# Second norm, choice of expert and scatter as one stage by batches of 1024 tokens, and gates chosen inside the second attention

## The reference

```python
probs = jax.nn.softmax(mla_out @ router_w + router_b, axis=-1)
topw, topi = jax.lax.top_k(probs, TOPK)                    # TOPK = 2
topw = topw / (topw.sum(-1, keepdims=True) + 1e-08)
combine = jnp.sum(jax.nn.one_hot(topi, E, dtype=probs.dtype) * topw[..., None], axis=-2)
h1 = jax.nn.gelu(jnp.einsum('bsd,edf->ebsf', mla_out, w1) + b1[:, None, None, :], approximate=False)
h2 = jnp.einsum('ebsf,efd->ebsd', h1, w2) + b2[:, None, None, :]
return hs + 0.3 * jnp.einsum('bse,ebsd->bsd', combine, h2)
```

```python
for i in range(E):
    wi = w_flat[:, i:i + 1]                                # 0 where expert i was not chosen
    h = jax.nn.relu(jnp.einsum('nd,hd->nh', x_flat * wi, w1[i]) + b1[i])
    y = jnp.einsum('nh,dh->nd', h, w2[i]) + b2[i]
    out = jnp.where(wi > 0, y, out)
```

## Time and profile before

| what | value |
|---|---|
| median of three runs | 1809.29 us |
| the profiled execution | 1809.21 us |
| its span, first to last instruction | 1807.4 us |
| granted TensorE clock, mean | 0.92 |
| busy: PE, DVE, ACT, POOL | 86%, 72%, 71%, 29% |

### The profile page before, as it was taken

The page is one execution under the profiler, slowest core; times in us unless marked ns, Lnnn a source line. Parts: engine busy times, 40 slices in busy tenths (PEclk is TensorE's granted clock), DMA queues, the critical chain, the costliest instruction groups (busy, mean ns, idle before and its releaser), DMA issues. The chain is left out here.

```text
span 1807.4 us, 38985 instructions
## 1 busy us (share of the span) xinstructions
PE 1558.9 (86%) x13976; PEld 841.3 (47%) x13976; DVE 1305.1 (72%) x1816; ACT 1274.6 (71%) x2406; POOL 524.2 (29%) x742
## 2 busy tenths in 40 slices
PE   5999999999979999999999999949999653672197
PEld 4555555555534444444344443337777221222187
DVE  3777777777679999999999999334555459655175
ACT  2777777777637998998899998838888477131177
POOL 0222222222144101100100111029989033113566
PEclk8999999999978999999999999879999866785599
DMA  2021100000013110010011000024554000022300
GB/s 79 22 87 52 52 21 19 17 18 17 17 31 111 26 27 4 13 31 10 5 30 34 16 25 4 1 45 100 83 83 71 15 0 0 0 111 76 97 30 32
DMA packets 40103, 68.40 MB, mean 38 GB/s; under 512 B 9192, under 2 KB 20208, under 8 KB 39472
## 3 DMA queue, kind: packets, MB, share of 16 engines
q1 hardware_dynamic: 34608, 59.87, 13.9%
q0 software_dynamic: 5376, 6.96, 1.4%
HBM read 32.56 MB, written 7.77 MB: 22 GB/s over the span
## 5 line engine op out<-in xcount | busy, mean ns | idle before, releaser
L903 ACT ACTIVATE m_probs<-m_ring 128x512 f32<-128x512 f32 x1024 | 543.3, 598 | 83.3 <-PE m_ring L825 67.8
L972 DVE TENSOR_REDUCE m_half_max<-m_pairs 128x2 f32<-128x1024 f32 x512 | 587.7, 1212 | 12.7 <-PE m_pairs L808 12.3
L387 DVE TENSOR_REDUCE a_neg_max<-a_scores 128x1 f32<-128x1024 f32 x257 | 310.4, 1214 | 91.1 <-PE a_scores L314 91.0
L375 ACT ACTIVATE a_probs<-a_scores,a_neg_max 128x1024 f32<-128x1024 f32 x256 | 285.1, 1114 | 123.5 <-DVE a_neg_max L387 123.5
L840 PE MATMUL m_acc<-m_probs,m_v_aug 128*32 128x256 f32 (+1 forms) x4032 | 330.7, 401 | 0.0
L825 PE MATMUL m_ring<-m_q_max,m_k 32*128 32x512 f32 x1024 | 319.6, 503 | 3.8 <-DVE m_q_max L986 2.9
L808 PE MATMUL m_pairs<-m_k,m_q 32*128 32x512 f32 x1024 | 264.1, 513 | 12.9 <-DVE m_half_max L972 9.6
L314 PE MATMUL a_scores<-a_q,a_k_own 64*128 64x512 f32 x516 | 260.1, 620 | 6.5 <-ACT a_probs L375 5.6
L314 PE MATMUL a_scores<-a_q,a_k_other 64*128 64x512 f32 x516 | 258.4, 620 | 0.7 <-ACT a_probs L375 0.2
L825 PEld LDWEIGHTS m_ring<-m_q_max,m_k 32*128 32x128 f32 x1024 | 146.5, 184 | 219.3 <-ACT m_probs L903 115.9
L422 POOL TENSOR_TENSOR a_scaled<-values,a_inv 128x128 f32<-128x128 f32 x256 | 102.1, 399 | 389.0 <-DVE a_inv L405 258.0
(11 more groups left out here) (257 smaller groups left out, 2097.7 us busy)
## 6 DMA issues: line engine op xcount, KB each, us to landing
e_gates<-sorted_results SPq DMA_DIRECT2D x64, 256.0 KB, 7.7
a_k_other<-a_k_own SPq DMA_DIRECT2D x66, 128.0 KB
m_k<-m_k_init SPq DMA_DIRECT2D x8, 512.0 KB, 3.9
m_q<-xT SPq DMA_DIRECT2D x8, 512.0 KB, 4.3
sorted_tokens<-q_blank SPq DMA_DIRECT2D x5, 544.0 KB, 6.4
f_records<-sorted_tokens SPq DMA_DIRECT2D x10, 272.0 KB, 4.9
e_w<-e_w_dram SPq DMA_DIRECT2D x1, 2064.0 KB, 8.1
xT<-x_t_dram SPq DMA_DIRECT2D x1, 2048.0 KB, 7.6
```

What stands on the lines that cost most here:

```text
L375: nc.scalar.activation(probs[:, g, :], scores[:, slot(h * G + g), :], ACT.Exp, bias=neg_max[:, g:g + 1], accum_out=total[:, g:g + 1]).then ...
L387: nc.vector.tensor_reduce(neg_max[:, i % G:i % G + 1], scores[:, slot(i), :], AX, ALU.max, negate=True).then_inc(max_done, 1)
L903: nc.scalar.activation(probs[:, u % SLOTS, head, :], ring[:, bank, :], ACT.Exp, scale=0.5).then_inc(ring_taken, 1)
L972: nc.vector.tensor_reduce(half_max[:, pair // PAIRS % 2, at:at + 2], pairs[:, pair % 2, :, :], AX, ALU.max).then_inc(pair_taken, 1)
```

## The change

- **Gates in the second attention.** A class `BestTwo` holds the choice. For the first 28 tiles it runs on VectorE after that engine's last pair of the attention; its exponential (item Y) and the high part of chunk 0 (item Z) are put into the last block on ScalarE. TensorE turns the gates of two chunks after the last weighing, and ScalarE and SyncE bring them to DRAM, before the last chunk's output is finished. `largest` now stands ahead of `split_weights` on GpSimd.
- **No routing block.** The last four tiles are chosen inside the first experts, in four pieces between the units of chunk 1.
- **`place_stage`** takes the place of norm "ln2" and sort. It steps through the chunks; after every second chunk VectorE chooses for 8 tiles (`choose`), and after the next step places them (`put`), so that GpSimd can scatter them. Each expert has a region of 4224 rows in DRAM, so a slot needs only the counts so far. The rows after each expert's last token are cleared by 8 DMAs at addresses in registers.
- **Loads of the last stage.** 40 DMAs of one tile, each after its address was read into a register of SyncE, in place of 10.

The diff's core, `routing_stage` and `sort_stage` (removed) left out:

```diff
@@ second_attention_order
+        if number + 1 == BLOCKS_ALL and u in (4, 6):
+            items.append(("Y Z"[u - 4], None, None))
@@ class BestTwo, on `tiles` tiles
+    def shift(self, dve, x, bias):
+        self.tt(x, x, self.row(bias), ALU.add)
+        self.reduce(self.m0, x, ALU.max)
+        self.tt(x, x, self.wide(self.m0), ALU.subtract)
+    def normalize(self):                      # 3 instructions
...
+    def pick_first(self, order):              # 5
...
+    def pick_second(self, order):             # 6
...
+    def gates(self, gate):                    # 6
...
+EARLY = TILES - 4
@@ second_attention_stage, TensorE after the last weigh
+                pe.wait_ge(gates_done, 1)
+                for c in range(ROWS_AHEAD):
+                    for t in range(4):
+                        last = nc.tensor.matmul(pairs[0:E, c, 0, t * TILE:(t + 1) * TILE], gate[:, 4 * c + t, :], ident,
+                                                start=True, stop=True)
+                    last.then_inc(gates_turned, 1)
@@ ScalarE
+                        elif kind == "Y":
+                            act.wait_ge(to_exp, 1)
+                            nc.scalar.activation(best.p, logits[:, 0:EARLY, :], ACT.Exp).then_inc(exped, 1)
+                        elif kind == "Z":
+                            nc.scalar.activation(x_first[:, 0, :], mla[:, S:S + BANK], ACT.Copy).then_inc(x_high_done, 1)
...
                 take_sums(f)
+                for c in range(ROWS_AHEAD):
+                    act.wait_ge(gates_turned, c + 1)
+                    nc.scalar.activation(ahead[:, c * BANK:(c + 1) * BANK], pairs[0:E, c, 0, :],
+                                         ACT.Copy).then_inc(rows_set, 1)
                 logarithms(f)
@@ VectorE
+                dve.wait_ge(ring_taken, by_scalar(UNIT_AT[BLOCKS_ALL - 1, "R"]))
+                best.shift(dve, logits[:, 0:EARLY, :], router[:, E:2 * E])
+                dve.sem_inc(to_exp, 1)
+                dve.wait_ge(exped, 1)
+                best.normalize()
+                best.pick_first(iota[:, E:2 * E])
+                best.pick_second(iota[:, E:2 * E])
+                best.gates(gate[:, 0:EARLY, :])
+                dve.sem_inc(gates_done, 1)
@@ experts_stage, VectorE
+                best.shift(dve, logits[:, EARLY:, :], router_bias)
+                dve.sem_inc(to_exp, 1)
                 for n in range(UNITS + U):
                     if n < UNITS:
                         weigh(n)
+                    if n == U:
+                        dve.wait_ge(exped, 1)
+                        best.normalize()
+                    if n == U + 2:
+                        best.pick_first(iota[:, E:2 * E])
+                    if n == U + 4:
+                        best.pick_second(iota[:, E:2 * E])
+                    if n == U + 6:
+                        best.gates(gate[:, EARLY:, :])
@@ place_stage, TensorE (turn: 4 matmuls of 8 columns and 4 transposes)
+                pe.wait_ge(order_in, 16)
+                for s in range(CH + 3):
+                    if s < CH:
+                        means(s)
+                    if 1 <= s <= CH:
+                        variances(s - 1)
+                    if s >= 4 and s % BATCH_CHUNKS == 0:
+                        rank(s // BATCH_CHUNKS - 2)
+                    if 2 <= s < CH + 2:
+                        turn(s - 2)
@@ ScalarE
+                for s in range(CH + 2):
+                    if s < CH:
+                        square(s)
+                    if 1 <= s <= CH:
+                        invert(s - 1)
+                    if s >= 2:
+                        copy(s - 2)
+                    if s >= 3 and s % BATCH_CHUNKS == 1:
+                        act.wait_ge(to_exp, s // BATCH_CHUNKS)
+                        nc.scalar.activation(p[:, :, :], x[:, :, :], ACT.Exp).then_inc(exped, 1)
@@ VectorE (choose: 25 instructions, put: 9, table: 14)
+                for s in range(CH + 3):
+                    if s < CH:
+                        centre(s)
...
+                    if s >= 4 and s % BATCH_CHUNKS == 0:
+                        put(s // BATCH_CHUNKS - 2)
+                    if 1 <= s <= CH:
+                        scale(s - 1)
+                    if s >= 3 and s % BATCH_CHUNKS == 1 and s // BATCH_CHUNKS <= B:
+                        choose(s // BATCH_CHUNKS - 1)
+                table()
@@ GpSimd
+                for b in range(B):
+                    pool.wait_ge(copied, BATCH_CHUNKS * (b + 1))
+                    pool.wait_ge(recorded, 3 + b)
+                    pool.wait_ge(slots_done, b + 1)
+                    for t in range(b * PER_BATCH, (b + 1) * PER_BATCH):
+                        nc.gpsimd.indirect_dma_start(scratch, bass.IndirectOffsetOnAxis(ap=slots[:, t:t + 1], axis=0),
+                                                     records[:, t, :], None).then_inc(scattered, 16)
@@ SyncE
+                sp.wait_ge(pads_known, 1)
+                for e in range(E):
+                    at = sp.value_load(pad_at[0:1, e:e + 1], min_val=0, max_val=E * REGION)
+                    sp.dma_start(scratch[ds(at, TILE), :], blank[:, e, :]).then_inc(padded_done, 16)
@@ sorted_experts_stage, SyncE
+                for t in range(SORT_TILES):
+                    at = sp.value_load(tile_base[0:1, t:t + 1], min_val=0, max_val=E * REGION + (SORT_TILES - 1) * TILE)
+                    sp.dma_start(records[:, t, :], scratch[ds(at, TILE), :]).then_inc(loaded[t // PER], 16)
                 for c in range(CHUNKS):
-                    sp.dma_start(records[:, c * PER:(c + 1) * PER, :],
-                                 scratch[c * PER * TILE:(c + 1) * PER * TILE, :].rearrange("(t p) d -> p t d", p=TILE)
-                                 ).then_inc(loaded[c], 16)
-                for c in range(CHUNKS):
-                    sp.wait_ge(loaded[c], 16)
+                    sp.wait_ge(loaded[c], 16 * PER)
```

More of the change, by code:

```diff
@@ L710, in second_attention_stage @@
+ROWS_AHEAD = 2
+EARLY = TILES - 4
+def second_attention_stage(core, xT, tiles, ident, bias_out, mla, router, logits, weights, iota, gate, gate_dram,
+                           x_first, loads):
     nc = core.nc
@@ new lines, in place_stage @@
+        counts, upto, earlier = (tmp(n, [TILE, E, PER_BATCH]) for n in ("counts", "upto", "earlier"))
+        start, count, padded, end, step_rows, ones = (tmp(n, [TILE, E]) for n in (
+            "start", "count", "padded", "end", "step_rows", "ones"))
+        over = tmp("over", [TILE, E, TILES])
+        passed, moved = tmp("passed", [TILE, TABLE, E]), tmp("moved", [TILE, TABLE, E])
+        expert, base = tmp("expert", [TILE, TABLE]), tmp("base", [TILE, TABLE])
+        eps_set = core.sem("p_eps_set")
@@ L1861, in _ @@
+                sp.wait_ge(padded_done, 16 * (E + 1))
+                sp.wait_ge(loaded, 16 * (len(loads) - 1))
             @block.tensor
             def _(pe):
-                for c, tiles in enumerate(GROUPS):
-                    if c >= RING:
-                        pe.wait_ge(copied, c - RING + 1)
-                        pe.wait_ge(biased, c - RING + 1)
-                    for n, t in enumerate(tiles):
-                        last = nc.tensor.matmul(turned[:, c % RING, n * WIDTH:(n + 1) * WIDTH],
-                                                src[:, t * TILE:(t + 1) * TILE], turning, start=True, stop=True)
-                    last.then_inc(turned_done, 1)
@@ new lines, in variances, with turn @@
+                def variances(c):
+                    pe.wait_ge(squared_done, c + 1)
+                    if c >= 2:
+                        pe.wait_ge(log_done, c - 1)
+                    nc.tensor.matmul(var[:, c % 2, :], mean_w, squared[:, c % 2, :], start=True,
+                                     stop=True).then_inc(var_done, 1)
+                def turn(c):
+                    pe.wait_ge(normed, c + 1)
+                    if c >= 2:
+                        pe.wait_ge(copied, c - 1)
+                    if c % BATCH_CHUNKS == 0 and c:
+                        pe.wait_ge(biased, c // BATCH_CHUNKS)
+                    for t in range(4):
+                        tile = dst[:, (4 * c + t) * TILE:(4 * c + t + 1) * TILE]
+                        at = (4 * c + t) % PER_BATCH * E
+                        nc.tensor.matmul(logits[:, at:at + E], tile, router[:, 0:E], start=True, stop=True)
+                        last = nc.tensor.transpose(turned[:, c % 2, t * TILE:(t + 1) * TILE], tile, ident)
+                    last.then_inc(turned_done, 1)
```

548 lines of the change are left out of this document (298 added, 250 removed).

## The result

| | runs shown with the result | median | profiled execution |
|---|---|---|---|
| before | 1805.27 to 1817.53 us (4) | 1808.77 us | 1809.21 us, span 1807.4 |
| changed | 1783.35 to 1793.16 us (4) | 1785.70 us | 1783.47 us, span 1781.6 |

The ratio is 0.9888, with a 95% interval from 0.9859 to 0.9916: 1.1% faster, some 20 us (15 to 26). The forecast was 1795.9 us with a range from 1784 to 1810; the time lies in it, near its lower end, and close to that of rival B, 1785.5. By the ratio it is faster by a little more than the 1% bound, to which I gave 0.36, though the interval reaches to 0.8%. The two profiled executions are 25.8 us apart.

What follows compares the result with a forecast made beforehand. TensorE bound the first experts; lone chains and GpSimd's scatters held other stretches. From 1809.2 us, 15.4 - 0.3 - 1.5 + 7.6 - 7.9 = 13.3 us gained gave 1795.9 us, range 1784 to 1810.

Steps and rivals of the forecast that it cites:

- rival B: Place stage: TensorE's clock stays up and the cycle is near 14 us, gaining about 18; time 1785.5 us; chance 0.22.
- The removed block: Gates chosen during the second attention, so the first experts begin earlier: 15.4 us gained, bounds 14.5 and 16.2.
- Y, Z and the copies: Second attention: Y and Z put 1.0 us on ScalarE, 0.3 lost (bounds 0 and 1.0); copies of turned gates cost nothing.
- The late choice: First experts, chunk 1: choosing for the last four tiles adds 20 VectorE instructions; 1.5 us lost, bounds 0 and 4.4.
- `largest` ahead of `split_weights`: GpSimd in the second attention: the swap only delays pieces needed 50 us later, and costs nothing.
- The place stage: Norm, choice and scatters in batches: 88.0 us in place of 95.6, gain 7.6; bounds gain 18, loss 6.5.
- The loads: Last stage: 8 register reads and DMAs at 1.2 us precede the first tile; cost 7.9 us, bounds 4.0 and 11.1.
- Rival S: Last stage: SyncE's loads become the bound, from about 2.2 us per tile; at 3.3 the time is 1833 us; chance 0.04.
- C: Last stage's loads: register reads overlap the DMA issue, 0.7 us per tile; 4 us better, 1792 us; chance 0.12.
- D: Place stage: TensorE stays at 1.2 GHz, loss 6.5 us in place of a gain of 7.6; time 1810; chance 0.11.
- P: Place stage: choices of three batches wait for 24 scatters of 0.96 us, 23 us; time 1819; chance 0.05.
- F: Second attention: the early choice is late or TensorE waits for gates, some 5 us lost; time 1801; chance 0.06.

Runs made afterwards that it cites:

- swap_only: The kernel before, with only GpSimd's order changed in the second attention, `largest` ahead of `split_weights`: 1805.67 us against 1809.57 (ratio 0.9985).

## Why the prediction was right or wrong

- **The removed block.** Right: 16.1 us, within the bounds of 14.5 to 16.2. The half clock at the start cost little: it rose within some 5 us. The choice in the last block was covered, but by less than I said: its last instruction ended at 1171.01, 0.5 us after the last weighing and not 3 before it. TensorE waited 0.58 us for the gates. The copies were done at 1173.66, 1.3 us before the divisors landed, so nothing behind moved. From chunk 6's logits to the last ones the changed kernel takes 24.95 us and `swap_only`, without the choice, 24.4 (1164.30 to 1188.68): 0.6 for Y, Z and the copies, where I took 0.3 within 0 to 1.
- **The late choice.** This step failed: 1.5 us, bounds 0 and 4.4, and 8.5 came. I priced 20 instructions at 0.22, from a row in which GpSimd idled, and put them where GpSimd is busy 173.71 of 193.70 us. The row that says otherwise stood in the text, 1.37 in place of 0.42, beside what was a subtraction and not an addition; I weighed it for the scatters alone, where it does not hold.
- **`largest` ahead of `split_weights`.** I said that it "only delays pieces that are needed 50 us later: nothing", and looked at what is delayed, not at what comes sooner. Before, TensorE waited 1.6 us for it and then worked at half clock, 2.9 to 5.0 us in all. The attention's 5.6 us are mostly the other fall of the clock, whose cause is open, so they bear out neither this term nor its opposite.
- **The place stage.** The mechanism was right: a chain, batches behind each other, scatters beside the next choice, the clearing and the table hidden. The sizes were too large by 9 us. The first scatter came 26.0 us after the start (28 and 0.95 for GpSimd's beginning forecast); two cycles took 15.07 and 15.06 and not 16.3. My 16.3 was 14.9 at full clock and 1.4 for the half clock; the one cycle at full clock took 13.38 and the half clock costs 1.7, so the sum of the instructions was 1.5 too large and the clock's price about right; and the last took 12.93, since of the norm only one scaling lies in it. That I had multiplied by three without looking at what the last cycle holds is the largest miss, 3.4 us. (39.25 over 31 is 1.266 per scatter and not 1.262, which changes nothing.)
- **The loads.** Right in kind, too dear: the second chunk was weighed 9.7 us after the first issue, ahead of which lies one register read, where I had 11.6 with it. The first activation came 13.3 us after the first issue in place of 7.6, and 4.7 us of that delay reached the end. Rival S is out: 1.1 us per tile stays far below the 2.2 at which SyncE would bind.
- **Rivals.** B gave the time, 1785.5, but not by its mechanism: its clock that stays up did not come, and the place stage's 16.7 was paid for by 8.5 in the experts and helped by an attention 5.6 us shorter. C's 0.7 per tile, D's loss and P's waiting choices did not come either: choice instructions took 0.22 us beside scatters, and scatters 0.96. F did not come: the early choice was early enough.

The forecast's sum was 13.3 us, and the two profiles lie 25.8 apart. The time fell within the range because a missed loss (7) cancelled part of the missed gains (9, 3 and the attention's 6). That is luck, and so is the closeness to rival B's number.

## What to carry to other kernels

Price a moved instruction from a row with the same neighbours: here VectorE's element-wise instructions of 4 to 32 elements cost some six times as much, and in one place twenty times, where they met GpSimd's arithmetic, and nothing extra where GpSimd waited or only issued DMAs. When a swap on one engine's queue is "free", ask who waits for the half that comes sooner, above all if TensorE does. In a row of cycles, work out the first and the last by themselves.

## What the runs showed of the hardware that I had not expected

- A VectorE tensor_tensor of 32 elements took 4.05 us beside GpSimd instructions of 1.26 us back to back, in six of six profiles, and 0.19 where GpSimd was idle; as scalar_tensor_tensor the same work took at most 1.28 (one profile).
- TensorE's clock fell to 0.50 while TensorE was busy throughout (before, 1160.9 us on), and stayed there for some 13 us.
- With the same code, the attention left half clock at 556 to 565 us or at 574 to 579; that alone moves the attention by about 6 us in the profiles. What decides it was not tried.
- Reading an address into SyncE's register and issuing the DMA took 1.10 to 1.15 us together, and ScalarE's queue did it at the same pace beside it (four issues start within 3.3 us).
